# A gather ring of eight groups of two rows instead of four groups of four

## What is computed

```python
q = (x @ Wq + bq).reshape(-1, 8, 128)
s1, s2 = einsum(q[..., :64], keys[:, 0]), einsum(q[..., 64:], keys[:, 1])
scores, best = top_k(all pairs of the top 8 of s1 and of s2, 8)
inner = einsum('bd,bhkd->bhk', x, w_down[indices])
vals = relu(inner) * softmax(scores)
out = einsum('bhk,bhkd->bd', vals, w_up[indices])
```

## Time and profile before

| | us |
|---|---|
| median of 3 runs | 1517.33 |
| lowest and highest | 1516.46, 1520.87 |
| span of the profiled execution | 1598.9 |
| first gather issued to last sum of the gather stage | 384 to 1446 |
| PE, DVE, POOL, ACT busy in the span | 1246.5, 979.1, 829.4, 335.6 |

### The profile page before, as it was taken

One profiled execution on the slowest core, in us unless ns is written; L12 is line 12 of the kernel. 1 busy time (PEld: TensorE's weight loads), 2 busy tenths in 40 slices (PEclk: granted clock), 3 DMA queues, 4 the chain that ended last, 5 costly groups with the idle time before them and its releaser, 6 DMA issues.

```text
span 1598.9 us, 17228 instructions
## 1 busy us (share of the span) xinstructions
PE 1246.5 (78%) x3954; PEld 604.1 (38%) x3955; DVE 979.1 (61%) x3058; ACT 335.6 (21%) x910; POOL 829.4 (52%) x921
## 2 busy tenths in 40 slices
PE   4787789974877877797778878867887878788468
PEld 1333345542422433444334334343343433233233
DVE  4777771127497586684864866747758678555501
ACT  0111110024322223232221222221222222220011
POOL 5777700002567566565555665655656656763112
PEclk9999999985899999899888989988989999999779
DMA  9200000003889889898888898887998989986153
GB/s 350 87 0 0 0 0 0 1 0 118 307 305 349 298 325 345 281 324 320 302 302 301 300 336 301 316 322 261 361 338 291 354 301 350 373 327 243 72 184 125
DMA packets 105746, 378.51 MB, mean 237 GB/s; under 512 B 11824, under 2 KB 11826, under 8 KB 104536
## 3 DMA queue, kind: packets, MB, share of 16 engines
q0 software_dynamic: 94720, 343.40, 59.3%
q1 hardware_dynamic: 10968, 34.48, 5.8%
HBM read 359.53 MB, written 19.41 MB: 237 GB/s over the span
## 4 chain that ended last, share of the span: by engine, by line
PE 47%; DVE 19%; issue 12%; ACT 5%; DVEq 5%; another core or an unknown queue 5%; DMA 5%; POOL 2%; POOLq 0%; SPq 0%; ACTq 0%
PE tr L1274 20%; DVE big L956 8%; PE acc L1171 5%; PE acc L1230 4%; PE acc L1131 4%; PE acc L1253 3%; PE tr L1326 2%; DVE topi L859 2%; DMA big<-in_wdu,idx 2%; ACT diag L642 2%; PE tr L1302 2%; PE acc L1201 2%; PE acc L1243 2%; DVEq L730 2%
## 5 line engine op out<-in xcount | busy, mean ns | idle before, releaser
L476 POOL DMA_INDIRECT big<-in_wdu,idx x640 | 641.8, 1003 | 587.0 <-issue 583.1
L1274 PE MATMUL tr<-big,diag 128*128 128x512 f32 x1280 | 650.1, 656 | 190.2 <-ACT diag L642 98.1
L956 DVE CUSTOM_DVE_ANT_0 big<-big,y 128x512 f32<-128x512 f32 x640 | 405.3, 689 | 129.9 <-DMA big<-in_wdu,idx 100.9
L1274 PEld LDWEIGHTS tr<-big,diag 128*128 128x128 f32 x1280 | 255.8, 209 | 536.4 <-issue 402.2
L642 ACT ACTIVATE diag<-ident,val 128x128 f32<-128x128 f32 x640 | 204.6, 393 | 604.7 <-DVE val L961 342.1
L1131 PE MATMUL acc<-outT 128*128 128x512 f16 (+1 forms) x612 | 126.1, 345 | 33.0 <-POOL outT L461 14.7
L461 POOL TENSOR_SCALAR outT<-gt,big 128x128 f16<-128x128 f16 x153 | 130.2, 864 | 21.8 <-PE acc L1131 10.9
L856 DVE MAX8 top<-acc 128x8 f32<-128x256 f32 x160 | 61.2, 424 | 109.8 <-PE acc L1243 97.9
L736 DVE TENSOR_SCALAR outT<-big 128x1250 f16<-128x1250 f16 x204 | 110.3, 595 | 17.6 <-PE acc L1131 12.1
L1230 PE MATMUL acc<-yT,qk 128*128 128x128 f32 x640 | 86.5, 301 | 25.3 <-ACT qT L621 24.7
L1253 PE MATMUL acc<-AT,gt 128*128 (+2 forms) x240 | 97.4, 529 | 4.2 <-DVE gt L840 3.2
(11 more groups left out here) (217 smaller groups left out, 782.1 us busy)
## 6 DMA issues: line engine op xcount, KB each, us to landing
sorted_rows<-big SPq DMA_DIRECT2D x8, 1280.0 KB, 17.9
big<-in_wdu,idx POOLq DMA_INDIRECT x640
big<-in_we SPq DMA_DIRECT2D x8, 1024.0 KB, 14.0
x<-sorted_rows SPq DMA_DIRECT2D x14, 512.5 KB, 3.5
x<-in_x SPq DMA_DIRECT2D x1, 2304.0 KB
qk<-in_wq SPq DMA_DIRECT2D x1, 2048.0 KB, 19.8
big<-in_w0t SPq DMA_DIRECT2D x1, 1024.0 KB, 28.2
qk<-in_keys SPq DMA_DIRECT2D x1, 1024.0 KB, 19.5
```

The costliest lines, as they stand in the source:

```text
L476: pool.indirect_dma_start(out=k.big[:, slot * 2 * D:(slot + 1) * 2 * D], out_offset=None, in_=k.wdu_d, in_offset=bass.IndirectOffsetOnAxis ...
L956: dve.tensor_tensor_reduce(out=k.big[:, slot:slot + D], in0=k.big[:, slot:slot + D], in1=k.y[:, par * D:(par + 1) * D], scale=1.0, scalar=0.0,
L1274: ins = pe.matmul(k.O[par], k.diag[:, c:c + P], k.big[:, slot:slot + D], start=(g == 0 and s == 0), stop=(g == NG - 1 and s == GS - 1))
```

## The change

```diff
-GS = 4
+GS = 2
 NG = HK // GS
-RING = 4
+RING = 8
```

```diff
-    k.diag = sb("diag", 2 * GS * P)
+    k.diag = sb("diag", 4 * GS * P)
```

## The result

The changed kernel takes 1599.3 us in the median of four runs (1595.9 to 1603.2), the kernel before beside it 1517.8 (1516.5 to 1520.9): 1.054 times as long, with an interval of 1.052 to 1.056, or 81.5 us more. In a second set of runs it was 1595.8 against 1519.3, a ratio of 1.051 (1.047 to 1.055).

What follows compares the result with a forecast made beforehand. It took the order of work among four waiting programs as the bound. Eight tiles added 59 us, the last tile took off 12 and the start 2.5: 45 us on 1517, so 1562 us, range 1500 to 1612.

Steps and rivals of the forecast that it cites:

- the half clock: Rival: PE falls to half clock more often, in bare groups and queries; 5 us a tile, 1602 us; chance 0.2.
- more unnamed waits: Rival: more waits like ACT's ahead of the query copies, 10 us each; one more in two tiles, 1602 us; chance 0.06.
- What bounds the kernel: No engine is full; order of work binds: PE in groups 2 to 5, DVE in 6 to 10, then both in turns.
- The price of a group: On DVE, drain, last accumulator and `val` cost 0.32 us a group; sixteen more groups add 5.1 us a tile.
- So gathers do not starve here: Bare groups 15 to 25: POOL's full ring keeps rows ahead, so PE's pace holds, 18.9 us.
- bare groups that follow POOL's 2.6 us instead of PE's 1.72: Sign, in groups without search or units, that the forecast is wrong; it expected them 1.72 us apart on PE.
- the early groups: Groups before 10: those bound by DVE lose 7.4 us, those bound by PE 6.9 and 0.6; 14.9 us less.
- Units: Groups 26 to 31, two units each: DVE and PE hand over in turn, 3.3 us a group, 19.8 for six.
- The first and the last tile: First tile, without units: about 0. Last tile, without search and limited by POOL: 11 to 12 us off.
- The sum: Eight tiles with search and units add 59 us, last tile takes 12 off, start 2.5: 45 us more.
- Carrying the difference over: The 45 us, reckoned on the profiled 1598.9 us, was added to the median 1517: 1562 us; span excess stays in both profiles.
- The finer ring: Rival: waits for landed rows are on the path and slots freed by twos remove them; 1452 to 1502 us; chance 0.18.

Runs made afterwards that it cites:

- spread search: The changed kernel with the search's pieces at twice their group number, units left two to a group; 1519.3 us beside 1519.3 for the kernel before, ratio 1.000.
- the experiment with the units alone: The changed kernel with only the units spread, one to a group in the last twelve groups; 1595.1 us beside 1595.8 for the changed kernel.
- the squeezed: The kernel before, groups of four, with the search's pieces at half their group number, two to a group; 1766.2 us beside 1610.9, ratio 1.098.
- even order: Groups of two with all search steps spread evenly and units one to a group in 20 to 31; 1712.0 us beside 1590.0 for the kernel before.
- later top eight: Search at twice its group numbers, DVE's first top eight three groups after PE's first scores instead of two; 1503.2 us beside 1518.7 for the kernel before.
- before with two `val`: The kernel before with a drain and a `val` after two slots and after four on DVE; 1609.6 us beside 1610.9, ratio 0.997.

## Why the prediction was right, and where it was not

The sign and the range held, and of the mechanism the part up to the search's end; the size was 45 us where 81 were measured. That 1599 us lay within the range owes something to its width: its upper part, up to 1612, was there for the half clock and for more unnamed waits, and neither of them made the time.

*What bounds the kernel.* Right. The stretch from y to the first scores is PE's, and in the profile of 1520.1 us it goes from y (1098.54) to the top eight (1122.43) in 23.9 us; after the change in 16.9 (1151.27 to 1168.18). I had said 7.5 less; it is 7.0. DVE's wait there was said to be some 10 us and is 9.75. The four groups that PE does in this stretch are 1 to 4, for it still has group 1 to do when y is ready; between the transpose and the first scores are only three, where I had written groups 2 to 5.

*The price of a group.* Too high: groups of two with their rows landed follow 1.46 us apart where I had 1.55, and the shortest distance of two groups of four is 2.69 us, in both profiles of the kernel before, where I had 2.78. From the first dot product to the end of `val` was no period, since the next dot product starts 0.09 us before that end. The price by the group is 2 x 1.46 - 2.69 = 0.23 us and not 0.32, 37 us in all where I had 51; DVE's busy time rose by 31.6 us. As a part of the loss it was wrong as well. I wrote that of 7.4 us a tile 5.1 were DVE's work by the group. The spread search shows the same work at no loss; what costs is that the work doesn't fit where it stands. For POOL I put the price at nothing but its sequencer's. Its 640 issues took 28.4 us longer, but no run shows this in the time of the search's tiles: the spread search has 40.9 us of it at no loss.

*"So gathers do not starve here."* This is the step that failed. Groups 15 to 25 took 24.3 us instead of 18.9. I had POOL's first wanted issue at group 22 at the moment the bare groups begin, and the crossing near group 27, with everybody at PE's pace. In fact a slot is freed by PE, and PE is some two groups behind DVE there: when DVE closes group 14, at 1207.2, PE is still at group 12 (1204.3 to 1207.9), and the gathers that take the slots of group 12 are those of group 20, the first of them issued at 1208.92. And DVE is not held to PE's pace: it takes a group each 1.46 us as long as rows are in the ring. The ring was dry for DVE at group 20, and from there a group took POOL's time, two issues, 2.5 us and more. The prediction had named this as a sign of being wrong: bare groups that follow POOL's 2.6 us instead of PE's 1.72. It held for groups 20 to 25. These 5.4 us are more than the 2.0 us by which the tile's sum was short (7.4 against 9.4 us): the early groups saved 2.2 us more than forecast, and groups 10 to 14 and 26 to 31 took 1.3 us less. Most of DVE's 96 us of waits for rows lie in this stretch.

*Units.* Right: 19.3 us for six groups against 19.8, and the experiment with the units alone shows that their place is free. It is free because two limits lie close together there, POOL's pace and PE's work with the units, and the spread units exchange the one for the other; the prediction had not seen that.

*The first and the last tile.* The first was right, about 0: its last matmul ends at 499.1 us after the change and at 498.3 before. The start gave nothing of the 2.5 us: DVE's first dot product starts at 396.0 us before and at 396.1 after. For the last I took 12 us off, out of the 90.0 us between POOL's first and last issue in the profile of 1598.9 us. The tile takes 85.1 us after the change, and took 82.1, not 90, in the profile of 1520.1 us. A term of -12 was one of +3; this is 15 us, the largest single error. It came from a stretch of a profile whose kernel took 1599 us, not 1518: the 7.5 us that I took for the ring's were not there at 1518 (its 64 gathers are issued in 82.6 us). After the change they are issued in 84.5, the issues themselves being longer.

*The sum.* Eight tiles with search and units: 59 us forecast, 73 measured (the ends of `val` of the tiles). Last tile -12, measured +3. Start -2.5, measured 0 to 1. That is 45 against 77, and outside the tiles there are 4 us more.

*Carrying the difference over.* I supposed that the 81.6 us between span and median were the profiler's and would stand in both profiles. They were not and did not: the span after is 1601.2 us against 1599.3. The tile was to take about 112 us in the profile and took 107.1, because it starts from 97.8 and not from 105. That its own sum came out near in spite of it is because I had added up instructions that follow each other, and not whole tiles: the eighth tile has such a wait too, 7.2 us of ACT at 1175 us, but beside a full PE.

*The rivals.* The finer ring gave no gain: with slots freed by twos and the search in its old place the time is the same to 0.2%. What the ring of eight would give without the added drains and the longer issues is not tested. The half clock is hardly a cause of the loss: the granted clock over the tiles is 0.93 after the change and 0.94 before, and of the 960 distances between neighbouring matmuls within fours of L1274 101 are over 0.6 us (full clock has 0.43) where 92 were before, some 4 us. But it does come with the squeezed and with the even order, at 0.87. More of the unnamed waits did not come either: there is none on any engine in the tiles of the profile after. The rule that I had weighed with them, that of the Trainium skill, Runtime: NRT & Kernel Launch, section Instruction fetch mechanics, is that a taken branch out of the window stalls; the loop is longer after the change, and the trace shows no added wait that could be laid to it.

## What to carry to other kernels

Where engines meet at hand-placed steps, the group number is a unit of time. Whoever halves the group must move with it every step that another engine waits for, and the distance between a producer's step and its consumer's is the slack that both have. Before a saving is sought in finer buffers, compare the same order with the finer groups: here they were free and gave nothing by themselves, and one group more between the first scores and the first top eight gave 1%. And a wait is no measure of what its removal gives: DVE's wait for rows fell by 68 us with the units spread, and the time stayed, because PE's work stood right behind it.

## What was not expected of the hardware

- Two profiles of the kernel before, with spans of 1598.9 and 1604.2 us, have 79.6 and 97.2 us of waits with an unnamed end ahead of ACT's copies of the queries; the third, with 1520.1 us, has none. What makes them no run tells.
- A gather's issue on POOL takes longer with groups of two: 1045 ns in the mean after the change, 1059 with the later top eight, and 1001 in groups of four (first line after, second before):

```profile
L476 POOL DMA_INDIRECT big<-in_wdu,idx x640 | 669.1, 1045 | 559.2 <-issue 426.0 <-PE tr L1274 118.4 <-DVE val L961 14.8
```
```profile
L476 POOL DMA_INDIRECT big<-in_wdu,idx x640 | 640.7, 1001 | 511.5 <-issue 507.3 <-DVE val L961 3.3 <-PE tr L1274 0.9
```

The longer issues of the changed kernel are those beside a `val` of two columns on DVE. Two issues of the eighth tile, the first with the `val` of 1155.34 us inside it, the second with DVE idle:

```profile
1154.92 1.16 POOL L476 DMA_INDIRECT big<-in_wdu,idx  x1 [0.30 <-issue]
...
1159.31 0.94 POOL L476 DMA_INDIRECT big<-in_wdu,idx  x1 [0.30 <-issue]
```

| mean of an issue, us (how many) | before (1520.1 us) | after | before with two `val` (1609.8 us) |
|---|---|---|---|
| beside an idle DVE | 0.944 (81) | 0.944 (65) | 0.944 (107) |
| beside a `val` | 0.955 (132) | 1.134 (306) | 1.132 (250) |
| beside other work of DVE | 1.026 (427) | 0.969 (269) | 0.958 (283) |

In the last column POOL has its groups of four and DVE the `val` of two columns, so it isn't the ring. It isn't the length of a row of issues either: in the last tile, where POOL issues all 64 with hardly a pause, the mean is 1.001 us before and 1.034 after. Why a `val` of two columns does this and one of four does not is not shown.
